# A recommender with two interaction layers: embedding rows stored chunk by chunk, a new order of the work ahead of the first product, and three top-layer products moved into the last two steps

## The reference, cut to what matters

```python
e = jnp.stack([tbl_0[ids[:, 0]], ..., tbl_31[ids[:, 31]]], axis=1)    # [1024, 32, 64]

def _cin_layer(h, h0, W, b):                                        # W: [128, Hn * 32]
    Wr = W.reshape(W.shape[0], Hn, Mn)
    x = jnp.einsum('bhd,bmd,ohm->bod', h, h0, Wr) + b[None, :, None]
    return jax.nn.relu(x)
x1 = _cin_layer(e, e, W1, b1)                                       # [1024, 128, 64]
next_hidden, direct1 = x1[:, :64], x1[:, 64:]
direct2 = _cin_layer(next_hidden, e, W2, b2)
z = jnp.sum(jnp.concatenate([direct1, direct2], axis=1), axis=-1)   # [1024, 192]
h = jnp.concatenate([z, dense_ctx], axis=1)                         # [1024, 208]
h = jnp.maximum(h @ W_top1 + b_top1, 0.0)                           # 208 x 512
h = jnp.maximum(h @ W_top2 + b_top2, 0.0)                           # 512 x 256
y = h @ W_top3                                                      # 256 x 1
```

## Time and profile before

| | us |
|---|---|
| median of 3 runs | 2058.44 (2058.43 to 2058.59) |
| the profiled execution's own time | 2057.63 |
| its span, first to last instruction | 2055.8 |
| TensorE busy | 2012.2 (98%) |
| VectorE busy | 1983.9 (96%) |
| ScalarE busy | 1631.9 (79%) |
| GpSimd busy | 1524.0 (74%) |

### The profile page before, as it was taken

The page is one execution under the profiler, slowest core; times in us unless marked ns, Lnnn a source line. Parts: engine busy times, 40 slices in busy tenths (PEclk is TensorE's granted clock), DMA queues, the critical chain, the costliest instruction groups (busy, mean ns, idle before and its releaser), DMA issues.

```text
span 2055.8 us, 28705 instructions
## 1 busy us (share of the span) xinstructions
PE 2012.2 (98%) x6890; PEld 1299.2 (63%) x6890; DVE 1983.9 (96%) x545; ACT 1631.9 (79%) x4755; POOL 1524.0 (74%) x580
## 2 busy tenths in 40 slices
PE   3899999999999999999999999999999999999999
PEld 1566666666666666666666666666666666666664
DVE  5999999999999999999999999999999999999992
ACT  2788788788888888887887887887887888888873
POOL 3877787787787787787787788778778777778520
PEclk9999999999999999999999999999999999999999
DMA  6777777776776776776776776776777777767740
GB/s 185 215 210 208 198 213 203 198 217 199 200 214 200 204 215 196 207 216 190 211 213 195 208 216 192 210 212 191 215 208 197 211 205 201 212 200 206 210 108 1
DMA packets 239331, 406.51 MB, mean 198 GB/s; under 512 B 33377, under 2 KB 50273, under 8 KB 239090
## 3 DMA queue, kind: packets, MB, share of 16 engines
q1 hardware_dynamic: 231026, 397.10, 66.7%
q0 software_dynamic: 8192, 8.40, 2.0%
HBM read 321.49 MB, written 16.78 MB: 165 GB/s over the span
## 4 chain that ended last, share of the span: by engine, by line
DVE 59%; issue 35%; PE 3%; DMA 1%; SPq 1%; ACT 0%; DVEq 0%; POOL 0%; ACTq 0%; POOLq 0%
DVE pnear L459 27%; DVE pfar L459 16%; DVE plo L464 16%; PE acc L521 0%; ACT phi L655 0%; PE acc L527 0%; PE acc L538 0%; PE x1p L586 0%; PE acc L586 0%; PE acc L528 0%; DMA near<-emb_rows 0%; POOL gathered L237 0%; DMA rem_b<-emb_rows 0%; SPq L301 0%; PE acc L592 0%
## 5 line engine op out<-in xcount | busy, mean ns | idle before, releaser
L237 POOL DMA_INDIRECT gathered<-in_tables,idx x256 | 762.0, 2977 | 104.8 <-issue 52.8
L258 POOL TENSOR_TENSOR prod<-near,h 128x2048 f32<-128x2048 f32 x126 | 577.2, 4581 | 174.4 <-PE acc L522 168.7
L655 ACT CAST phi<-pnear 128x4096 fp32r<-128x4096 f32 x128 | 465.9, 3640 | 269.9 <-DVE pnear L459 269.9
L527 PE MATMUL acc<-phi,w2lo 128*128 128x512 f32 x1536 | 603.9, 393 | 14.3 <-ACT phi L655 14.3
L528 PE MATMUL acc<-phi,w2hi 128*128 128x512 f32 x1536 | 603.1, 393 | 0.0
L602 ACT ACTIVATE acc<-acc,bias 128x64 f32<-128x64 f32 (+1 forms) x2048 | 574.9, 283 | 11.7 <-PE acc L528 8.5
L464 DVE TENSOR_TENSOR plo<-pnear,phi 128x4096 fp32r<-128x4096 f32 x128 | 571.8, 4467 | 2.0 <-ACT phi L655 2.0
L459 DVE TENSOR_TENSOR pfar<-far,x1p 128x4096 f32<-128x4096 f32 x128 | 565.8, 4420 | 6.9 <-PE acc L538 1.1
L459 DVE TENSOR_TENSOR pnear<-near,x1p 128x4096 f32<-128x4096 f32 x128 | 564.9, 4414 | 4.7 <-ACT x1p L638 4.7
L521 PE MATMUL acc<-prod,w1T 128*128 128x512 f32 x1024 | 462.5, 594 | 14.3 <-DVE prod L444 12.9
L538 PE MATMUL acc<-pfar,w2T 128*128 128x512 f32 x1024 | 460.3, 592 | 0.0
(11 more groups left out here) (68 smaller groups left out, 535.5 us busy)
## 6 DMA issues: line engine op xcount, KB each, us to landing
near<-emb_rows SPq DMA_DIRECT2D x512, 256.0 KB
far<-emb_rows SPq DMA_DIRECT2D x512, 256.0 KB, 4.2
x1rep<-x SPq DMA_DIRECT2D x256, 256.0 KB, 4.2
h<-emb_rows SPq DMA_DIRECT2D x128, 256.0 KB
emb_rows<-gathered SPq DMA_DIRECT2D x128, 128.0 KB, 3.5
gathered<-in_tables,idx POOLq DMA_INDIRECT x256, 4.9
rem_a<-emb_rows SPq DMA_DIRECT2D x64, 64.0 KB, 3.6
rem_b<-emb_rows SPq DMA_DIRECT2D x64, 64.0 KB, 3.0
```

Source lines behind the costliest of these rows:

```text
L237: nc.gpsimd.indirect_dma_start(out=gathered[s][:, g, :], out_offset=None, in_=a["tables"], in_offset=bass.IndirectOffsetOnAxis(ap=idx[s][: ...
L258: nc.gpsimd.tensor_tensor(prod1[:, :, :], near[(u + 2) % 3][:, :, :], h0[odd][:, :].unsqueeze(1).to_broadcast([P, K1, N]), ALU.mult).then_ ...
L527: nc.tensor.matmul(acc2[s][:, :], w2lo[:, t, :], phi[:, t, :], start=(t == 0), stop=False)
L655: nc.scalar.copy(phi[:, 0:T_NEAR, :], pnear[:, :, :, :].rearrange("p a k n -> p (a k) n")).then_inc(hi_near_ready, 1)
```

## The change

Three things are changed together.

First, `emb_rows` becomes one block per chunk: 64 rows of 512 floats, contiguous. `near` and `far` are loaded with one DMA each in which a partition reads four consecutive rows (8 KB); partition (i, q) of tile k now holds field i + 4q + k. The weights' diagonals, the order of the ids and the table offsets follow from that (table offsets come in two small loads, ids are cast in two halves).

Second, the order ahead of the first steps. VectorE waits for `idx_ready` 2, which GpSimd raises after the four lookups of pair 0, before it starts on the weights. The dense inputs are turned and copied ahead of W2's blocks. VectorE's first product is made in two halves, and TensorE starts on the first half. The turns of W2 stand behind the first product, two of them behind the second. ScalarE, not VectorE, makes w2hi. TensorE runs four extra matmuls ahead of the first product and three ahead of step 0, with results that nobody reads. SyncE loads near(0) first, and near(2) and the second remainder ahead of replicating x1.

Third, the top layer's products 0 to 2 are issued in the last two steps, one in step 126 and two in step 127, in the place of the layer-1 product that these steps don't have; the third and fourth PSUM buffer of the top layers are in x1p[0], not x1p[1].

```diff
-ROW = B * D + 1024
+CHUNK = 2 * F * N
-        emb = nc.dram_tensor("emb_rows", [2 * F, ROW], fp32, kind="Internal")
+        emb = nc.dram_tensor("emb_rows", [CHUNKS, CHUNK], fp32, kind="Internal")
-        top_acc = [acc1[0], acc1[1], tp[0], tp[1]]
+        top_acc = [acc1[0], acc1[1], x1p[0][:, 0:N], x1p[0][:, N:2 * N]]
-        LOADS = 16 * (1 + K1)
+        LOADS = 16 * 2
-            return bass.AP(base.tensor, base.offset, [list(base.ap[0]), [SH, K1], [65, F], [1, SH]])
+            return bass.AP(base.tensor, base.offset, [list(base.ap[0]), [1, K1], [65, F], [SH, SH]])
...
-            sp.dma_start(table_row[:, :], a["table_rows"]).then_inc(ids_in, 16)
+            for half in range(2):
+                sp.dma_start(table_row[half * P // 2:(half + 1) * P // 2, :],
+                             a["table_rows"].rearrange("(f half q) one -> half f q one", half=2, q=SH // 2)[half]).then_inc(ids_in, 16)
...
-                for k in range(K1):
-                    src = bass.AP(emb, SH * k * ROW + col, [[ROW, F], [ROW, SH], [1, N]])
-                    sp.dma_start(near[s3][:, k, :], src).then_inc(near_in[s3], 16)
+                sp.dma_start(near[s3][:, :, :].rearrange("p k n -> p (k n)"),
+                             bass.AP(emb, c * CHUNK, [[N, F], [SH * N, SH], [1, K1 * N]])).then_inc(near_in[s3], 16)
+            def load_far(c, s):
+                sp.dma_start(far[s][:, :, :].rearrange("p k n -> p (k n)"),
+                             bass.AP(emb, c * CHUNK + HALF * N, [[N, F], [SH * N, SH], [1, K2 * N]])).then_inc(far_in[s], 16)
...
             store_rows(0, 0, 1)
             sp.wait_ge(emb_stored, STORES)
+            load_near(0, 0, 0)
             load_rem(0)
-            load_near(0, 0, 0)
+            load_near(1, 1, 1)
             load_far(0, 0)
-            load_near(N, 1, 1)
             store_rows(1, 1, 1)
+            sp.wait_ge(emb_stored, 2 * STORES)
+            sp.wait_ge(tp_copied, 2)
+            sp.wait_ge(p1_ready, 1)
+            load_near(2, 0, 2)
+            sp.wait_ge(rem_prod_ready, 1)
+            load_rem(2)
             sp.wait_ge(x1_ready, 1)
             replicate_x1()
             sp.wait_ge(w2_wide, 1)
             sp.wait_ge(w2_second, 1)
-            load_far(N, 1)
-            sp.wait_ge(emb_stored, 2 * STORES)
-            sp.wait_ge(rem_prod_ready, 1)
-            load_rem(2 * N)
-            sp.wait_ge(tp_copied, 2)
-            sp.wait_ge(p1_ready, 1)
-            load_near(2 * N, 0, 2)
+            load_far(1, 1)
...
@@ vector
             dve.wait_ge(w1_in, 16)
+            dve.wait_ge(idx_ready, 2)
...
-            dve.wait_ge(tp_filled, 3)
-            nc.vector.tensor_copy(flat(w2T[:, :, :]), tp[0][:, :]).then_inc(tp_copied, 1)
-            for h in range(T_SPLIT // K1):
+            dve.wait_ge(top_zero, 1)
+            for h in range(2):
+                dve.wait_ge(tp_filled, 3 + h)
+                nc.vector.tensor_copy(z1[0:DENSE, h * N:(h + 1) * N], tp[h][0:DENSE, :]).then_inc(tp_copied, 1)
+            def low_weights(h):
                 hi, lo = (flat(w[:, K1 * h:K1 * (h + 1), :]) for w in (w2hi, w2lo))
-                dve.wait_ge(tp_filled, 4 + h)
-                nc.vector.tensor_copy(hi, tp[1 - h % 2][:, :]).then_inc(part_hi, 1)
                 dve.wait_ge(part_hi, h + 1)
                 nc.vector.tensor_tensor(lo, tp[1 - h % 2][:, :], hi.bitcast(fp32), ALU.subtract).then_inc(tp_copied, 1)
...
+            dve.wait_ge(near_in[0], LOADS)
+            products1(0, slice(0, K1 // 2)).then_inc(p1_first, 1)
+            products1(0, slice(K1 // 2, K1)).then_inc(p1_ready, 1)
...
-            products1(0)
             dve.wait_ge(acc1_ready, 1)
-            products1(1)
+            dve.wait_ge(near_in[1], LOADS)
+            products1(1, slice(0, K1)).then_inc(p1_ready, 1)
+            dve.wait_ge(tp_filled, 5)
+            nc.vector.tensor_copy(flat(w2T[:, :, :]), tp[0][:, :]).then_inc(tp_copied, 1)
+            for h in range(T_SPLIT // K1):
+                low_weights(h)
...
@@ tensor
+            for h in range(2):
+                turn(2 + h, *DENSE_TURNS[h])
+            def keep_running(count):
+                for _ in range(count):
+                    nc.tensor.matmul(acc2[1][:, :], w1T[:, 0, :], flat(w1T[:, 0:N // O, :]), start=True, stop=True)
...
+            keep_running(4)
+            pe.wait_ge(p1_first, 1)
+            tiles1(0, range(0, K1 // 2))
+            pe.wait_ge(p1_ready, 1)
+            tiles1(0, range(K1 // 2, K1))
             pe.wait_ge(rem_lo_ready, 1)
-            for c in range(2):
-                pe.wait_ge(p1_ready, c + 1)
-                layer1(c)
+            remainder1(0)
+            pe.wait_ge(far_staged, 1)
+            turn(4, *FAR_TURNS[1])
+            pe.wait_ge(near_staged, 1)
+            turn(5, *NEAR_TURNS[0])
+            pe.wait_ge(p1_ready, 2)
+            layer1(1)
+            turn(6, *NEAR_TURNS[1])
+            turn(7, *FAR_TURNS[0])
+            keep_running(3)
...
+                elif at == CHUNKS - 2:
+                    pe.wait_ge(top_in, 16 * TOP_DMAS)
+                    pe.wait_ge(tp_copied, N_TURNS)
+                    pe.wait_ge(z1_ready, CHUNKS - 1)
+                    pe.wait_ge(z2_ready, CHUNKS // 2)
+                    top1(0)
+                else:
+                    pe.wait_ge(z1_ready, CHUNKS)
+                    top1(1)
+                    pe.wait_ge(pfar_ready, CHUNKS - 1)
+                    top1(2)
...
+            for n in range(3, 2 * M1):
+                if n >= M1:
+                    pe.wait_ge(z2_ready, CHUNKS)
+                if n >= len(top_acc):
+                    pe.wait_ge(top_ready, n - len(top_acc) + 1)
+                top1(n)
...
@@ scalar
+            def high_weights(h):
+                act.wait_ge(tp_filled, 6 + h)
+                nc.scalar.copy(flat(w2hi[:, K1 * h:K1 * (h + 1), :]), tp[1 - h % 2][:, :]).then_inc(part_hi, 1)
             remainder_hi(0)
             act.wait_ge(small_in, 16 * SMALL_DMAS)
             act.wait_ge(acc1_ready, 1)
             hidden1(0)
+            for h in range(T_SPLIT // K1):
+                high_weights(h)
             direct1(0, 0)
```

More of the change, by code:

```diff
@@ L140, in build_dlrm @@
         part_hi = sem("part_hi")
+        p1_first = sem("p1_first")
         tp_filled = sem("tp_filled")
@@ L361, in step @@
                     sp.wait_ge(rem_prod_ready, pair + 2)
-                    load_rem((c + 3) * N)
+                    load_rem(c + 3)
                 if within(at, 3):
@@ L381, in _ @@
         def _(dve):
-            dve.wait_ge(ids_in, 32)
-            nc.vector.tensor_copy(ids_f[:, :, :].rearrange("r g (f q) -> r g f q", q=GS),
-                                  ids_n[:, :, :, :].rearrange("r q g f -> r g f q")).then_inc(ids_float, 1)
+            dve.wait_ge(ids_in, 48)
+            for half in range(2):
+                last = nc.vector.tensor_copy(
+                    ids_f[:, :, half * P // 2:(half + 1) * P // 2].rearrange("r g (f q) -> r g f q", f=F),
+                    ids_n[:, half * GS // 2:(half + 1) * GS // 2, :, :].rearrange("r q g f -> r g f q"))
+            last.then_inc(ids_float, 1)
             dve.wait_ge(ids_turned, 1)
@@ L426, in _, with products1 @@
             nc.vector.tensor_copy(flat(w1remT[:, :, :]), tp[1][0:3 * REM, 0:2 * P]).then_inc(tp_copied, 1)
[L427 to L429 removed]
+            dve.wait_ge(top_zero, 1)
[3 more added lines that the diff above has]
+            def low_weights(h):
                 hi, lo = (flat(w[:, K1 * h:K1 * (h + 1), :]) for w in (w2hi, w2lo))
[L431 to L432 removed]
                 dve.wait_ge(part_hi, h + 1)
                 nc.vector.tensor_tensor(lo, tp[1 - h % 2][:, :], hi.bitcast(fp32), ALU.subtract).then_inc(tp_copied, 1)
[L435 to L445 removed]
+            def products1(s, ks):
+                return nc.vector.tensor_tensor(prod1[:, ks, :], near[s][:, ks, :],
+                                               h0[s][:, :].unsqueeze(1).to_broadcast([P, len(range(K1)[ks]), N]), ALU.mult)
+            dve.wait_ge(near_in[0], LOADS)
+            products1(0, slice(0, K1 // 2)).then_inc(p1_first, 1)
+            products1(0, slice(K1 // 2, K1)).then_inc(p1_ready, 1)
             dve.wait_ge(rem_in, 32)
@@ L473, in step @@
                 products2(pnear[:, :, :, :], near[u % 3][:, :, :], odd, K1).then_inc(pnear_ready, 1)
-                dve.wait_ge(far_in[odd], 16 * K2 * (turn * (U // 2)) + 16 * K2 * (u // 2 + 1))
+                dve.wait_ge(far_in[odd], 16 * (turn * (U // 2)) + 16 * (u // 2 + 1))
                 if begun(at):
@@ L508, in _, with top1, tiles1, remainder1 @@
             turn(1, *REM_TURN)
-            pe.wait_ge(far_staged, 1)
-            turn(2, *FAR_TURNS[1])
-            pe.wait_ge(near_staged, 1)
-            for h in range(A2):
-                turn(3 + h, *NEAR_TURNS[h])
-            turn(5, *FAR_TURNS[0])
+            def top1(n):
+                h, m = n // M1, n % M1
```

(31 more changed lines are left out.)

28 lines of the change are left out of this document (7 added, 21 removed).

## The result

The changed kernel takes 2098.61 us (median of 5, 2096.29 to 2100.66) against 2058.43: a ratio of 1.0199, 95% interval 1.0185 to 1.0213. I had forecast 2052.0, faster. The profiled execution took 2100.66 us, its span is 2098.9, 43.1 us longer than before.

The account below looks back on a forecast made before the run. TensorE, busy in all 15.35 us of a step, was taken as the bound. Gains of 4.8 us (head) and 1.6 us (tail) sum to 6.4: 2058.44 - 6.4 = 2052.0 us, range 2048.5 to 2056.0.

Parts of the forecast that it names:

- the loads begin at 16.8 instead of 19.67: Head, lookups: last lookup starts at 11.45 instead of 14.29, then the old 2.52 us and 2.86 us follow.
- SP waits for nobody's sake in the loop, hence nothing: Main loop, chunk-major rows: one DMA for four cuts SP's issue from 2.54 to 0.6 us per tile; value zero.
- The sum: Whole kernel: 4.8 us gained by step 0 plus 1.6 us in the tail, 6.4 us in all; chunk-major rows zero.
- My slower rival: Main loop: chunk loads at twice today's time make DMA engines the bound, 490 us more, 2540 in all; chance 0.08.
- step 0 at 52.17 (52.3 forecast): End of the head: TensorE starts step 0 at 52.3 instead of 55.47.
- gap-free running: After the head: TensorE runs without a gap from 58.15 instead of 62.95, 4.8 us gained.
- a step of 15.35 us: Main loop: TensorE never pauses and its instructions stay the same, so one chunk still takes 15.35 us.
- 25.59 us in the tail: Tail: start of step 127 to second top layer takes 25.6 us instead of 27.2; 1.6 us gained.
- idle times of 1.1 and 1.5 us: Tail, TensorE: 1.1 us of idling left before step 127, and 1.5 us new before top product 4.
- The x1 copy: Head, ScalarE: copy starts at 43.2 (before 43.62), after direct1; x1 replica, requested at 32.8, in by 38.
- At the first product: Head, TensorE: near load lands 23.1 to 23.5, extra matmuls take 5.6 us to 28.4, product ends 32.1 instead of 37.7.
- 1.46 and 2.38 us did not bring the clock down: Tail, TensorE: idling that long had left the clock up, so 1.1 us should too; the 16 matmuls take 3.8 us.

Follow-up runs that it names:

- the cut stores: Also called the spread version: the changed kernel with each 128-partition store cut into two of 64 partitions, slowest DRAM dimension 64 instead of 2; 2050.05 us.
- the layout with cut stores: The kernel before with chunk-major rows and each store cut into two of 64 partitions, old head and tail; 2057.34 us.
- the version that replicates x1 first: The spread version with x1 replicated ahead of the loads of near(2) and the second remainder, and ScalarE's x1 copy ahead of direct1; 2049.25 us.

## Why the prediction was wrong

**The step that failed** is "With the old 2.52 us to the store and 2.86 us from store to first load, the loads begin at 16.8 instead of 19.67". The 2.52 held: the last lookup starts at 11.06 and the store at 13.63. The 2.86 was taken from a store with another access pattern, and I treated it as a property of the bytes. It became 7.87, the loads began at 21.50, and step 0 at 59.95 instead of 52.3. With the cut stores it was 3.95.

**The step that carried the price** is "SP waits for nobody's sake in the loop, hence nothing". The sum put at nothing what came to 40.0 us. I had counted SyncE's issue time and not its waits: the remainder's load stands behind `emb_stored`, and that wait had been 1.5 us in all only because the stores landed early. I bounded the DMAs by their throughput, 74% of the engines, where a landing some 1.2 us late was enough. The late remainder then found VectorE with 0.15 us of slack per step (15.35 less 15.20). The kernel before already showed the collision (5.26 us for a small GpSimd subtraction at 57.59); I used it in the head and did not ask where it could come back in the loop.

**My slower rival** had the wrong mechanism. It asked for loads of 1.5 times today's cost, with the DMA engines as the bound. Their share fell instead (0.65, before 0.71), and the layout with cut stores costs nothing (2057.34). The fault was in the write side, which none of my cases looked at.

**What was right**, read on the version with the cut stores, where the failed step is removed: step 0 at 52.17 (52.3 forecast), gap-free running from 57.33 (58.15), a step of 15.35 us, 25.59 us in the tail (25.6), idle times of 1.1 and 1.5 us there.

**What came out by luck.** The x1 copy started at 43.01 (43.2 forecast), but its row ends in 1.31 us of waiting for the replica, which I had put in by 38: ScalarE was ready earlier than forecast, and the replica, requested at 35.5 and not at 32.8, came later. Step 0 and the gap-free start rest on that copy. At the first product two terms were off against each other: VectorE could start on the near tile only at 25.75, not at 23.5, and the extra matmuls took 4.6 us, not 5.6. The product began at 27.03 instead of 28.4, and not because of the extra matmuls, since it began at 27.04 without them. The time, 2050.05, is 2 us below the forecast: 0.8 of it is the earlier gap-free start and 0.8 the distance between profiled and timed median which I had added and which this version doesn't show (2050.01 and 2050.05); 0.4 is left. Two sums were also off by 0.1 to 0.2 us and decide nothing: 52.3 + 6.0 is 58.3 and not 58.15, and 2027.5 + 6.9 is 2034.4 and not 2034.6.

## What to carry to other kernels

When an access pattern changes, take its duration from no older row before comparing the slowest dimensions of both sides: a leading 2 can leave 14 of 16 DMA engines idle, and a small share of busy DMA engines in the stretch of one transfer (13.1% here) shows it. For every wait that costs nothing today, ask how late its releaser may come and what the work behind it would then run beside. Here a GpSimd product of 1.3 us that came 1.2 us later in the median cost 40 us, since VectorE had 0.15 us of slack per step and the two exclude each other.

## What the runs showed of the hardware that was not expected

The granted clock is not decided by the length of the last idle time alone. After the same 1.51 us, behind the same transposes, the second layer-1 product ran at full speed in the spread version (3.70 us, the first row) and slowly in the version that replicates x1 first (5.40 us at 33.50, shown above), where the stretch table has a granted clock of 0.58:

```profile
33.63 3.70 PE L540 MATMUL acc<-prod,w1T 128*128 128x512 f32 x8 [1.51 <-DVE prod L450]
...
33.50:36.00 2.50, 2.50 (x4) 1.11 (x5) 1.15 (x2) 0.00 (x0) 0.00 (x0) 0.58 0.95 165
```

My forecast had taken "1.46 and 2.38 us did not bring the clock down" as a rule; it is not one. What decides it is not shown here: each version was traced once.
